# A GAT layer's softmax weights go through a PSUM bank, and two of its small PSUM regions become one

## The chip, the cores and the metric

The kernel runs on one core of a Trainium2 chip. The metric is device time in microseconds (us) from one launch to its end. The engines are TensorE (PE, with its weight loads as PEld), VectorE (DVE), ScalarE (ACT), GpSimd (POOL) and SyncE (SP). Each runs its own instructions in order, and they meet in semaphores.

## The reference

Four graph layers run one after the other over 6,250 nodes of 256 features and 100,000 edges sorted by destination. The change is in layer 0, a GAT layer of 8 heads:

```
h = einsum('nf,fhd->nhd', x, W);  a_src = sum(h*att_src, -1);  a_dst = sum(h*att_dst, -1)
e = leaky_relu(a_src[src] + a_dst[dst], 0.2)
e_exp = exp(e - segment_max(e, dst)[dst]);  denom = segment_sum(e_exp, dst)
alpha = e_exp / (denom[dst] + 1e-16)
out = segment_sum(h[src] * alpha[:, :, None], dst);  x = layernorm(x + relu(out + bias))
```

Layers 1 to 3 (two GCN convolutions, a weighted sum, a four-head attention) follow and are not touched.

## The kernel before, in words

**Steps and groups.** The edges are cut into 832 steps of 128 edges (one per partition), and 16 steps make a group; there are 52 groups. In layer 0 GpSimd gathers a step's 128 rows of 264 numbers from the table `tab_h0` with one indirect DMA (L1031) into a ring of 48 rows, `rows0` in `reg_x`. A row is 256 features, 8 source scores (columns `FEAT:ROW0`) and a one. The DMA of step t waits for the product of step t - 48.

**A step.** VectorE multiplies the 256 features by the 8 weights, each over 32 features (L1354). TensorE multiplies a one-hot 128x128 matrix by the row (L1312, two passes in fp32, written `bank<-reg_x,scratch`) into one of four product banks. VectorE adds that bank to the sums of the node tile (L1337), three steps behind. TensorE may so be up to three steps behind VectorE, and needs the add of step i - 4 before product i.

**The chain.** While a group's 16 steps go on, the weights of the next group are made in small pieces written out by hand, at step k = 0 to 15 of the running group (`chain_scalar`, `chain_tensor`, `chain_vector`):

- k = 0: VectorE caps the source scores (L1210). ScalarE makes the masks (L1091) and the first four one-hots (L1073, L1076; again at k = 2, 4, 5).
- k = 1 to 4: TensorE turns the scores (`turned3`, L1170), ScalarE copies them (L1121), VectorE makes the first running maxima (L1214), TensorE turns their ends (`tails`, L1174, L1175), ScalarE copies those (L1126). Between them TensorE turns the one-hots, four at a time (L1149), ScalarE copies them (L1085), and TensorE multiplies them with the destination scores (`dst0` to `dst3`, L1161).
- k = 6: VectorE carries the maxima from step to step (L1225 to L1238), ScalarE arranges them (L1134 to L1136).
- k = 7: TensorE turns those starting values and spreads the level (`begins`, L1194 and L1196), then does `dst2`; at k = 8 `dst3`. At k = 8 ScalarE copies two columns of it (`begin_col`, L1102), at k = 10 the destination scores (`part`, L1107).
- k = 11: VectorE's second scans (L1241, L1243) start from `begin_col`; then the node's value (L1248), a maximum (L1255) and L1258. At k = 12 TensorE turns that maximum (`larger`, L1178).
- k = 13, 14: VectorE adds `part` (L1262, L1265) and subtracts (L1276, `below`). At k = 14 ScalarE's Exp writes the 128x128 weights into the rows' columns `FEAT:ROW0` (L1114, `weights`). VectorE's multiplies of the next group wait for that.

**PSUM.** There are eight banks: four for products, two for turned one-hots (`bank_t`), one shared by the turned scores (`bank_3`) and the destination scores (`bank_d`), and `psum[7]` for the small transposes and the level (`bank_c`). Finished node tiles are divided, normalised and stored among the steps (`close_vector`, `close_scalar`).

Of the kernel before, what the change touches and what calls it, by code (L numbers as in the profile page):

```python
# [13 lines left out]
P = 128  # L14
NODES = 6250
EDGES = 100000
FEAT = 256
# [242 lines left out]
def build(nc, io):  # L260
    ctx = ExitStack()
    with ctx:
# [82 lines left out]
        s_weighted, s_scaled = signal("rows_weighted"), signal("sums_scaled")  # L345
        s_denscaled = signal("denominators_scaled")
        s_chain = {n: signal(f"{n}_chain") for n in ("vector", "tensor", "scalar")}
        s_far, s_hot4 = signal("distance_made"), signal("four_hots_made")
        s_mixed, s_reverse = signal("message_mixed"), signal("reverse_scaled")
        s_mean, s_bias, s_residual = signal("mean_made"), signal("bias_added"), signal("residual_added")  # L350
# [533 lines left out]
        S, H, D = GROUP, HEADS0, HEAD0_DIM  # L884
        W0_ROW = FEAT + H + 1
        BANKS0, LAG0 = 4, 3
        rows0 = reg_x[:, 0:3 * S * W0_ROW].rearrange("p (s f) -> p s f", f=W0_ROW)
        hots0 = reg_a[:, 0:2 * S * P].rearrange("p (s f) -> p s f", f=P)
        hots_t = reg_a[:, 2 * S * P:2 * S * P + 1024].rearrange("p (s f) -> p s f", s=2)
# [13 lines left out]
        step_masks, tails, states, begins = (cut(2 * P, rows=1) for _ in range(4))  # L903
        assert at_b[0] <= 7488
        level = small[0:1, 400:400 + 4 * H].rearrange("p (k f) -> p k f", k=2)
        bank_t, bank_3, bank_d, bank_c = (psum[4], psum[5]), psum[6][:, 0:3 * P], psum[6][:, 3 * P:4 * P], psum[7]

        h0_a = a_order.named("middle_clear start_clear end_clear")
        h0_v = v_order.named("level begins ones src_less src_below src_at")
        h0_p = p_order.named("src_idx")  # L910
        src_below = reg_w[:, 1280:1280 + POSITIONS]
# [76 lines left out]
        def close_scalar(e, i):  # L988
# [15 lines left out]
            "capped first over_in back_states states level_in level_out second_up second node bent_node larger below_node "  # L1004
            "part_added larger_added shrink_less bent shrink below", GROUPS)
        ch_t = s_chain["tensor"].named(
            "turned3 hots0 hots1 dst0 tails hots2 dst1 hots3 begins dst2 dst3 larger", GROUPS)
        ch_a = s_chain["scalar"].named(
            "upright hot0 kept3 hot1 kept_hot0 step_masks hot2 kept_tails kept_hot1 hot3 begins kept_hot2 kept_hot3 "
            "begin_col part shrink weights", GROUPS)  # L1010
# [54 lines left out]
        def chain_scalar(e, g, k, ahead):  # L1065
# [21 lines left out]
            if ahead:  # L1087
                if k == 0:
                    if g:
                        e.wait_ge(*ch_t.at("turned3", g - 1))  # L1090
                    e.copy(upright[:, 0:2 * P].rearrange("p (k s h) -> p k s h", k=2, h=H),  # L1091
                           bcast(masks[:, :, cols], 3, [P, 2, S, H])).then_inc(*ch_a.done("upright"))
                if k in (0, 2, 4, 5):
                    hot((0, 2, 4, 5).index(k))
                if k == 3:
                    if g:
                        e.wait_ge(*ch_v.at("level_out", g - 1))
                    e.copy(step_masks.rearrange("p (k h s) -> p k h s", k=2, h=H),
                           bcast(run_masks[:, :, cols], 2, [1, 2, H, S])).then_inc(*ch_a.done("step_masks"))
                if k == 8:  # L1100
                    e.wait_ge(*ch_t.at("begins", g))
                    e.copy(begin_col, bank_c[:, 256:258]).then_inc(*ch_a.done("begin_col"))  # L1102
                if k == 10:
                    e.wait_ge(*ch_t.at("dst3", g))
                    if g:
                        e.wait_ge(*ch_v.at("larger_added", g - 1))
                    e.copy(dst_part, bank_d[:, 0:S * H]).then_inc(*ch_a.done("part"))  # L1107
                if k == 11:
                    e.wait_ge(*ch_v.at("below_node", g))
                    e.activation(shrink0, shrink0, ACT.Exp).then_inc(*ch_a.done("shrink"))  # L1110
                if k == 14:
                    e.wait_ge(*ch_v.at("below", g))
                    e.wait_ge(*h0_v.at("ones"))
                    e.activation(group0(g)[0][:, :, FEAT:ROW0], both[:, 0:P].rearrange("p (s h) -> p s h", h=H),  # L1114
                                 ACT.Exp).then_inc(*ch_a.done("weights"))
                return
# [24 lines left out]
        def chain_tensor(e, g, k, ahead):  # L1141
# [23 lines left out]
            if ahead:  # L1165
                if k == 1:
                    e.wait_ge(*ch_a.at("upright", g))
                    e.wait_ge(*ch_v.at("capped", g))
                    for n in range(3):
                        t = e.transpose(bank_3[:, n * P:(n + 1) * P], upright[:, n * P:(n + 1) * P], ident[:, :])  # L1170
                    t.then_inc(*ch_t.done("turned3"))
                if k == 4:
                    e.wait_ge(*ch_v.at("first", g))
                    e.transpose(bank_c[0:1, 0:P], first[:, P - 1:P], ident[:, :])  # L1174
                    e.transpose(bank_c[0:1, P:2 * P], first[:, P:P + 1], ident[:, :]).then_inc(*ch_t.done("tails"))  # L1175
                if k == 12:
                    e.wait_ge(*ch_v.at("larger", g))
                    e.transpose(bank_c[:, 3 * P:4 * P], second[:, 0:P], ident[:, :]).then_inc(*ch_t.done("larger"))  # L1178
                return
            if k == 1:  # L1180
                turn_hots(0)
# [6 lines left out]
            if k == 6:  # L1188
                turn_hots(3)
            if k == 7:  # L1190
                e.wait_ge(*ch_a.at("begins", g))
                e.wait_ge(*h0_v.at("begins"))
                for n in range(2):
                    e.transpose(bank_c[:, 256 + n:257 + n], begins[:, n * P:(n + 1) * P], ident[0:1, 0:1])  # L1194
                e.wait_ge(*ch_v.at("level_in", g))
                e.matmul(bank_c[:, 264:264 + 2 * H], ones_row, level[:, g % 2, :], start=True,  # L1196
                         stop=True).then_inc(*ch_t.done("begins"))
                dst_scores(2)
            if k == 8:
                dst_scores(3)  # L1200

        def leaky(e, v):
            return e.scalar_tensor_tensor(out=v, in0=v, scalar=0.2, in1=v, op0=ALU.mult, op1=ALU.max)
# [1 line left out]
        def chain_vector(e, g, k):  # L1205
# [33 lines left out]
            if k == 11:  # L1239
# [5 lines left out]
                                     ALU.max).then_inc(*ch_v.done("second"))  # L1245
                load_ranks(e, "vector", g * S)
                v = rank_value(e, "vector", g * S)
                e.tensor_tensor(node_both.rearrange("p (k h) -> p k h", k=2),  # L1248
                                bank_c[:, 264:264 + 2 * H].rearrange("p (k h) -> p k h", k=2),
                                bcast(adst[:, bass.DynSlice(v * H, H)], 1, [P, 2, H]),  # L1250
# [9 lines left out]
            if k == 13:  # L1260
# [1 line left out]
                e.tensor_tensor(both[:, 0:P], upright[:, 2 * P:3 * P], dst_part,  # L1262
                                ALU.add).then_inc(*ch_v.done("part_added"))
                e.wait_ge(*ch_t.at("larger", g))
                e.tensor_tensor(both[:, P:2 * P], bank_c[:, 3 * P:4 * P], dst_part,  # L1265
                                ALU.add).then_inc(*ch_v.done("larger_added"))
                e.wait_ge(*ch_a.at("shrink", g))
                e.tensor_scalar(shrink0, shrink0, -1.0, carried[:, g:g + 1], ALU.add,
# [48 lines left out]
        def heads_vector(e):  # L1317
# [24 lines left out]
                            ALU.mult).then_inc(*h0_v.done("src_below"))  # L1342
            e.wait_ge(*h0_v.at("src_below"))
            e.tensor_tensor(src_at_i, src_at, src_below, ALU.add).then_inc(*h0_v.done("src_at"))
            for k in range(S):
                chain_vector(e, 0, k)
            e.wait_ge(*pre_p.at("rest_clear"))
            e.wait_ge(*h0_a.at("end_clear"))
            for i in range(STEPS_PAD):
                g, k = i // S, i % S  # L1350
                row = rows0[:, i % (3 * S), :]
                v = row[:, 0:FEAT].rearrange("p (h d) -> p h d", h=H)
                e.wait_ge(*ch_a.at("weights", g))
                e.tensor_tensor(v, v, bcast(row[:, FEAT:ROW0], 2, [P, H, D]), ALU.mult).then_inc(*weighted0.up)  # L1354
                if g + 1 < GROUPS:
                    chain_vector(e, g + 1, k)
                if i >= LAG0:
                    add(i - LAG0)
                close_vector(e, i)
            for i in range(STEPS_PAD, STEPS_PAD + LAG0 + 16):  # L1360
                if i < STEPS_PAD + LAG0:
                    add(i - LAG0)
# [903 lines left out]
```

## Time and profile before

| | us |
|---|---|
| median of 3 runs | 5281.45 (5277.9 to 5286.8) |
| the profiled execution's own time | 5284.91 |
| its span in the profile | 5283.1 |
| PE busy | 3888.6 (74%) |
| DVE busy | 3504.2 (66%) |
| ACT busy | 2567.7 (49%) |
| POOL busy | 3861.1 (73%) |

The span runs from the first to the last instruction. In the profile "busy" leaves out register and semaphore work, "idle before" is an engine's idle time just ahead of an instruction with what ended it, and L1354 is line 1354 of the kernel. Layer 0's steps lie between about 138 and 1207 us.

### The profile page before, as it was taken

Reading aid. Unit: us, or ns where it says so; the run is one execution under the profiler, and the core shown is the slowest. Engines: PE = TensorE matmul, PEld = TensorE weight load, DVE = VectorE, ACT = ScalarE, POOL = GpSimd, SP = SyncE. Lnnn points to the kernel's source line nnn. Section 1 sums busy time; section 2 is a strip of 40 time slices with the busy share of each in tenths; the row PEclk is TensorE's granted clock in tenths of the full one; section 3 lists DMA queues with packets and bytes.
Section 4 is the critical chain, followed back from the end, with each engine's and each line's share of the span. In section 5 each row is a group of like instructions: output and inputs, shape, how many; then the busy total and the mean of one; then the engine's idle time right before and its main releaser. Section 6 shows DMA issues by size and latency. Waiting matters only on the chain.

```text
span 5283.1 us, 86663 instructions
## 1 busy us (share of the span) xinstructions
PE 3888.6 (74%) x13357; PEld 2393.2 (45%) x13357; DVE 3504.2 (66%) x10780; ACT 2567.7 (49%) x6941; POOL 3861.1 (73%) x3995
## 2 busy tenths in 40 slices
PE   7888888886777777677777777676777657666663
PEld 5666666663444444344434434343334334444442
DVE  5889888885555455354444445666666578888887
ACT  3667666674555555355555551000000166666665
POOL 3777777766777777677777776777777777777775
PEclk8889889898998999777787787878887777777776
DMA  6444444433333333443333333333333322222222
GB/s 171 117 123 123 123 122 122 124 108 106 110 112 111 112 111 112 127 133 112 113 112 111 112 112 100 109 109 109 109 110 109 97 57 57 57 57 57 57 57 67
DMA packets 252627, 549.14 MB, mean 104 GB/s; under 512 B 71467, under 2 KB 136235, under 8 KB 252108
## 3 DMA queue, kind: packets, MB, share of 16 engines
q0 software_dynamic: 178752, 478.34, 33.3%
q1 hardware_dynamic: 45804, 42.37, 2.6%
q10 hardware_dynamic: 27552, 22.89, 1.5%
q8 instruction: 157, 2.57, 0.2%
q14 instruction: 362, 2.97, 0.2%
HBM read 501.16 MB, written 42.15 MB: 103 GB/s over the span
## 4 chain that ended last, share of the span: by engine, by line
POOL 55%; issue 20%; PE 10%; ACT 6%; DVE 4%; DMA 2%; SPq 1%; DVEq 0%; ACTq 0%; POOLq 0%
POOL scratch L1416 41%; POOL scratch L1886 14%; PE bank L1312 5%; PE bank L1161 3%; ACT scratch L1073 2%; DMA scratch<-tab_x,src_idx 1%; DVE reg_acc L1337 1%; PE bank L1149 1%; ACT scratch L1085 1%; DVE reg_x L1354 1%; SPq L872 1%; ACT scratch L1076 1%; DMA scratch<-tab_h,src_idx 1%; POOL reg_x L1031 0%; ACT scratch L1121 0%
## 5 line engine op out<-in xcount | busy, mean ns | idle before, releaser
L1468 PE MATMUL bank<-scratch 128*128 x4986 | 1904.2, 495 | 761.6 <-SPq L1428 407.3
L1478 DVE TENSOR_TENSOR reg_acc<-reg_acc,bank 128x256 f32 x2493 | 1048.1, 420 | 1361.7 <-PE bank L1468 1298.4
L1416 POOL DMA_INDIRECT scratch<-tab_x,src_idx x1566 | 1491.5, 952 | 533.3 <-issue 469.4
L1468 PEld LDWEIGHTS bank<-scratch 128*128 128x128 f32 x4986 | 964.3, 228 | 1602.9 <-issue 1549.0
L1031 POOL DMA_INDIRECT reg_x<-tab_h,src_idx x832 | 831.6, 1000 | 291.0 <-issue 176.7
L1416 POOL DMA_INDIRECT scratch<-tab_h,src_idx x783 | 744.4, 951 | 260.7 <-issue 234.3
L1886 POOL DMA_INDIRECT scratch<-tab_h,src_idx x783 | 741.2, 947 | 248.6 <-issue 237.7
L1937 PE MATMUL bank<-reg_w,scratch 128*128 128x260 f32 x1664 | 637.5, 527 | 286.6 <-issue 185.2
L1437 ACT ACTIVATE scratch<-iota_row,dst_loc 128x128 f32<-128x128 f32 x1662 | 572.1, 392 | 348.2 <-PE bank L1468 333.9
L1312 PE MATMUL bank<-reg_x,scratch 128*128 128x265 f32 x1664 | 577.8, 458 | 73.3 <-DVE reg_x L1354 71.1
L1937 PEld LDWEIGHTS bank<-reg_w,scratch 128*128 128x128 f32 x1664 | 377.3, 253 | 509.7 <-issue 312.1
L1968 ACT ACTIVATE edge_w<-scratch,attr 128x68 f32 x832 | 288.5, 347 | 311.1 <-SPq L1898 281.9
L1312 PEld LDWEIGHTS bank<-reg_x,scratch 128*128 128x128 f32 x1664 | 302.9, 215 | 203.6 <-DVE reg_x L1354 172.1
L1337 DVE TENSOR_TENSOR reg_acc<-reg_acc,bank 128x265 f32 x832 | 355.3, 427 | 45.8 <-PE bank L1312 35.3
L2054 DVE TENSOR_TENSOR reg_acc<-reg_acc,bank 128x260 f32 x832 | 350.3, 421 | 16.1 <-PE bank L1937 3.6
L1354 DVE TENSOR_TENSOR reg_x<-reg_x 128x256 f32<-128x256 f32 x832 | 344.6, 414 | 0.5 <-ACT reg_x L1114 0.5
L1453 DVE TENSOR_SCALAR scratch<-iota_row,dst_loc,edge_w 128x128 f32<-128x128 f32 x831 | 322.3, 389 | 6.1 <-issue 6.1
L1952 ACT ACTIVATE scratch<-iota_row,dst_loc 128x128 f32<-128x128 f32 x832 | 319.8, 386 | 3.4 <-DMA tab_h<-reg_w 1.6
L1787 ACT ACTIVATE adst<-adst,small 128x1 f32<-128x1 f32 x49 | 14.4, 294 | 611.2 <-DVE adst L1830 611.2
L2037 DVE SCALAR_TENSOR_TENSOR reg_w<-scratch,attr,edge_w 128x68 f32<-128x68 f32 x832 | 237.8, 286 | 95.0 <-ACT edge_w L1968 83.4
L2085 DVE TENSOR_TENSOR reg_w<-reg_w,bank 128x520 f32<-128x520 f32 x416 | 286.2, 688 | 0.5
L1442 ACT ACTIVATE scratch<-scratch 128x512 f32<-128x512 f32 x416 | 261.7, 629 | 13.1
(314 smaller groups left out, 4374.9 us busy)
## 6 DMA issues: line engine op xcount, KB each, us to landing
scratch<-tab_x,src_idx POOLq DMA_INDIRECT x1566, 2.8
scratch<-tab_h,src_idx POOLq DMA_INDIRECT x1566, 2.7
reg_x<-tab_h,src_idx POOLq DMA_INDIRECT x832
tab_h<-scratch ACTq DMA_DIRECT2D x7, 924.0 KB, 6.4
reg_x<-in_x SPq DMA_DIRECT2D x7, 896.0 KB, 11.3
reg_w<-in_x SPq DMA_DIRECT2D x49, 128.0 KB, 2.5
tab_x<-reg_acc SPq DMA_DIRECT2D x49, 128.0 KB
tab_xs<-reg_w SPq DMA_DIRECT2D x49, 128.0 KB, 2.7
```

What stands on the lines that cost most here:

```text
L1031: e.indirect_dma_start(rows0[:, t % (3 * S), 0:ROW0], None, tab_h0, bass.IndirectOffsetOnAxis(ap=src_idx[:, t:t + 1], axis=0)).then_inc(*g ...
L1312: e.matmul(psum[i % BANKS0][:, 0:W0_ROW], hots0[:, i % (2 * S), :], rows0[:, i % (3 * S), :], start=True, stop=True).then_inc(*product0.up)
L1337: e.tensor_tensor(v, v, psum[i % BANKS0][:, 0:W0_ROW], ALU.add).then_inc(*added0.up)
L1354: e.tensor_tensor(v, v, bcast(row[:, FEAT:ROW0], 2, [P, H, D]), ALU.mult).then_inc(*weighted0.up)
L1416: e.indirect_dma_start(ring_rows[:, j % SLOTS, :], None, self.table, bass.IndirectOffsetOnAxis(ap=src_idx[:, j:j + 1], axis=0)).then_inc(* ...
L1437: e.activation(ring_hots[:, i % HOTS, :], iota_row[:, :], ACT.Abs, scale=-1.0, bias=dst_loc[:, i:i + 1]).then_inc(*self.far.up)
L1453: e.tensor_scalar(ring_hots[:, i % HOTS, :], iota_row[:, :], dst_loc[:, i:i + 1], edge_w[:, i:i + 1], ALU.is_equal, ALU.mult).then_inc(*se ...
L1468: e.matmul(self.bank(i), ring_hots[:, i % HOTS, :], rows, start=True, stop=True).then_inc(*self.product.up)
L1478: e.tensor_tensor(v, v, self.bank(i), ALU.add).then_inc(*self.added.up)
L1886: e.indirect_dma_start(ring_rows[:, j % SLOTS, 0:ROW3], None, tab_h3, bass.IndirectOffsetOnAxis(ap=src_idx[:, j:j + 1], axis=0)).then_inc( ...
L1937: e.matmul(psum[i % BANKS][:, 0:WIDE3], hots3[:, i % HOTS, :], scaled3[:, i % 4, :], start=True, stop=True).then_inc(*product3.up)
L2054: e.tensor_tensor(v, v, psum[i % BANKS][:, 0:WIDE3], ALU.add).then_inc(*added3.up)
```

## The change

The weights of a group are copied by VectorE (`move_weights`) into `psum[7]`, in one of two halves, at the end of the group before, and the 16 multiplies read them there. The copy that Exp left in the rows stays, for the product's weight columns. The chain's small results move from `psum[7]` to `psum[6]`, the bank that already holds `bank_3` and `bank_d`. With that TensorE does `begins` after `dst3` at k = 8 and no longer before `dst2` at k = 7, ScalarE takes `begin_col` at k = 9, and VectorE waits for ScalarE's `part` ahead of L1248.

```diff
+        weights0 = psum[7][:, 0:2 * S * H].rearrange("p (g s h) -> p g s h", g=2, h=H)
-        bank_t, bank_3, bank_d, bank_c = (psum[4], psum[5]), psum[6][:, 0:3 * P], psum[6][:, 3 * P:4 * P], psum[7]
+        bank_t, bank_3, bank_d, bank_c = (psum[4], psum[5]), psum[6][:, 0:3 * P], psum[6][:, 3 * P:4 * P], psum[6]
...
-                if k == 8:
+                if k == 9:
                     e.wait_ge(*ch_t.at("begins", g))
                     e.copy(begin_col, bank_c[:, 256:258]).then_inc(*ch_a.done("begin_col"))
...
-                    e.transpose(bank_c[:, 3 * P:4 * P], second[:, 0:P], ident[:, :]).then_inc(*ch_t.done("larger"))
+                    e.transpose(bank_c[:, 0:P], second[:, 0:P], ident[:, :]).then_inc(*ch_t.done("larger"))
...
             if k == 7:
+                dst_scores(2)
+            if k == 8:
+                dst_scores(3)
                 e.wait_ge(*ch_a.at("begins", g))
...
-                dst_scores(2)
-            if k == 8:
-                dst_scores(3)
...
                 v = rank_value(e, "vector", g * S)
+                e.wait_ge(*ch_a.at("part", g))
                 e.tensor_tensor(node_both.rearrange("p (k h) -> p k h", k=2),
...
+            def move_weights(g):
+                e.wait_ge(*ch_a.at("weights", g))
+                if g >= 2:
+                    e.wait_ge(*weighted0((g - 1) * S - 1))
+                e.tensor_copy(weights0[:, g % 2], group0(g)[0][:, :, FEAT:ROW0]).then_inc(*moved0.up)
+
             for k in range(S):
                 chain_vector(e, 0, k)
+            move_weights(0)
...
-                e.wait_ge(*ch_a.at("weights", g))
-                e.tensor_tensor(v, v, bcast(row[:, FEAT:ROW0], 2, [P, H, D]), ALU.mult).then_inc(*weighted0.up)
+                e.wait_ge(*moved0(g))
+                e.tensor_tensor(v, v, bcast(weights0[:, g % 2, k, :], 2, [P, H, D]), ALU.mult).then_inc(*weighted0.up)
...
                 close_vector(e, i)
+                if k == S - 1 and g + 1 < GROUPS:
+                    move_weights(g + 1)
```

## Rows read from the trace of the kernel before

**Rows 1.** Page, costliest groups: busy us, mean ns of one, idle before it:

```profile
span 5283.1 us, 86663 instructions
...
L1478 DVE TENSOR_TENSOR reg_acc<-reg_acc,bank 128x256 f32 x2493 | 1048.1, 420 | 1361.7 <-PE bank L1468 1298.4
...
L1031 POOL DMA_INDIRECT reg_x<-tab_h,src_idx x832 | 831.6, 1000 | 291.0 <-issue 176.7
...
L1886 POOL DMA_INDIRECT scratch<-tab_h,src_idx x783 | 741.2, 947 | 248.6 <-issue 237.7
...
L1354 DVE TENSOR_TENSOR reg_x<-reg_x 128x256 f32<-128x256 f32 x832 | 344.6, 414 | 0.5 <-ACT reg_x L1114 0.5
```

**Rows 2.** Who waited, 140 to 1160 us: us in total, times, longest:

```profile
POOL reg_x L1031 <- issue: 163.0, 535, 0.3
...
DVE scratch L1225 <- ACT scratch L1126: 54.0, 37, 3.4
DVE reg_acc L1337 <- PE bank L1312: 35.1, 44, 1.8
DVE scratch L1210 <- DMA reg_x<-tab_h,src_idx: 13.0, 7, 3.2
DVE scratch L1265 <- PE bank L1178: 11.8, 17, 0.9
DVE reg_acc L1337 <- DVE reg_acc L1331: 7.3, 48, 0.2
...
ACT reg_x L1114 <- DVE scratch L1276: 136.8, 48, 4.6
ACT scratch L1107 <- PE bank L1161: 96.6, 43, 4.2
...
PE bank L1312 <- DVE reg_x L1354: 64.0, 127, 2.0
```

**Rows 3.** Windows: busy us (instructions) of PE, PEld, DVE, ACT, POOL, then granted clock:

```profile
140.00:1160.00 1020.00, 870.81 (x4427) 644.10 (x4425) 871.74 (x3125) 703.09 (x1879) 781.56 (x783) 0.89 0.45 122
505.50:525.50 20.00, 15.71 (x91) 11.38 (x90) 17.64 (x64) 14.06 (x42) 15.43 (x16) 1.00 0.54 145
239.20:263.20 24.00, 20.67 (x91) 15.23 (x90) 17.97 (x67) 14.07 (x40) 18.52 (x19) 0.79 0.51 140
```

**Rows 4.** Timeline, 517.7 to 525.3 us, a group at full clock, engine by engine:

```profile
517.76 0.28 PE L1194 MATMUL bank<-ident,scratch 1*128 1x1 f32 x2
...
518.20 1.06 PE L1161 MATMUL bank<-adst,scratch 128*128 x8
...
524.13 0.71 PE L1312 MATMUL bank<-reg_x,scratch 128*128 128x265 f32 x2 [0.90 <-DVE reg_x L1354]
...
518.31 0.16 ACT L1102 COPY scratch<-bank 128x2 f32<-128x2 f32 x1
520.64 0.27 ACT L1107 COPY scratch<-bank 128x128 f32<-128x128 f32 x1 [2.17 <-PE bank L1161]
...
519.65 0.48 DVE L1241 TENSOR_TENSOR_SCAN scratch<-scratch 128x128 f32<-128x128 f32 x1
```

**Rows 5.** Timeline, 253 to 263.5 us, a group at mostly half clock:

```profile
253.51 0.47 DVE L1241 TENSOR_TENSOR_SCAN scratch<-scratch 128x128 f32<-128x128 f32 x1
...
255.81 0.43 DVE L1337 TENSOR_TENSOR reg_acc<-reg_acc,bank 128x265 f32 x1 [0.88 <-PE bank L1312]
...
258.41 0.43 DVE L1337 TENSOR_TENSOR reg_acc<-reg_acc,bank 128x265 f32 x1 [1.50 <-PE bank L1312]
...
260.19 0.29 DVE L1265 TENSOR_TENSOR scratch<-bank,scratch 128x128 f32<-128x128 f32 x1 [0.75 <-PE bank L1178]
...
257.20 0.27 ACT L1107 COPY scratch<-bank 128x128 f32<-128x128 f32 x1 [4.24 <-PE bank L1161]
```

**Rows 6.** Timeline, 519.9 to 541 us: two gathers, and the VectorE instruction beside each:

```profile
524.83 0.95 POOL L1031 DMA_INDIRECT reg_x<-tab_h,src_idx  x1 [0.30 <-issue]
524.86 0.43 DVE L1337 TENSOR_TENSOR reg_acc<-reg_acc,bank 128x265 f32 x1
...
540.26 0.42 DVE L1354 TENSOR_TENSOR reg_x<-reg_x 128x256 f32<-128x256 f32 x1
540.35 1.15 POOL L1031 DMA_INDIRECT reg_x<-tab_h,src_idx  x1 [0.30 <-issue]
```

More of the change, by code:

```diff
@@ L347, in build @@
         s_chain = {n: signal(f"{n}_chain") for n in ("vector", "tensor", "scalar")}
+        s_moved = signal("weights_moved")
         s_far, s_hot4 = signal("distance_made"), signal("four_hots_made")
@@ L905, in build @@
         level = small[0:1, 400:400 + 4 * H].rearrange("p (k f) -> p k f", k=2)
-        bank_t, bank_3, bank_d, bank_c = (psum[4], psum[5]), psum[6][:, 0:3 * P], psum[6][:, 3 * P:4 * P], psum[7]
+        bank_t, bank_3, bank_d, bank_c = (psum[4], psum[5]), psum[6][:, 0:3 * P], psum[6][:, 3 * P:4 * P], psum[6]
         h0_a = a_order.named("middle_clear start_clear end_clear")
+        moved0 = s_moved.take(GROUPS)
         h0_v = v_order.named("level begins ones src_less src_below src_at")
@@ L1006, in build @@
         ch_t = s_chain["tensor"].named(
-            "turned3 hots0 hots1 dst0 tails hots2 dst1 hots3 begins dst2 dst3 larger", GROUPS)
+            "turned3 hots0 hots1 dst0 tails hots2 dst1 hots3 dst2 dst3 begins larger", GROUPS)
         ch_a = s_chain["scalar"].named(
@@ L1264, in chain_vector @@
                 e.wait_ge(*ch_t.at("larger", g))
-                e.tensor_tensor(both[:, P:2 * P], bank_c[:, 3 * P:4 * P], dst_part,
+                e.tensor_tensor(both[:, P:2 * P], bank_c[:, 0:P], dst_part,
                                 ALU.add).then_inc(*ch_v.done("larger_added"))
@@ L1350, in heads_vector @@
                 g, k = i // S, i % S
-                row = rows0[:, i % (3 * S), :]
-                v = row[:, 0:FEAT].rearrange("p (h d) -> p h d", h=H)
-                e.wait_ge(*ch_a.at("weights", g))
-                e.tensor_tensor(v, v, bcast(row[:, FEAT:ROW0], 2, [P, H, D]), ALU.mult).then_inc(*weighted0.up)
+                v = rows0[:, i % (3 * S), 0:FEAT].rearrange("p (h d) -> p h d", h=H)
+                e.wait_ge(*moved0(g))
+                e.tensor_tensor(v, v, bcast(weights0[:, g % 2, k, :], 2, [P, H, D]), ALU.mult).then_inc(*weighted0.up)
                 if g + 1 < GROUPS:
```

## The prediction, made before the changed kernel was run

> **What bounds the kernel now.** I read the page first, for what layer 0 is made of, then the waits, the windows and two timelines. The reader is to see which engine is late where, since the change touches layer 0 alone and the other 4,000 us stay.
>
> GpSimd looks like the bound of layer 0. Its 832 gathers take 1000 ns each [rows 1], and it never sits idle for more than 0.3 us between two [rows 2]: about 1.3 us a step, 16 x 1.3 = 20.8 us a group. But VectorE waits for gathered rows only 7 times, 13.0 us in all [rows 2]. So rows mostly lie ready when they are asked for, and the ring is not full either. The steps themselves go at nearly the same pace: one group took 20.0 us at full clock, one 24.0 us at a granted clock of 0.79 [rows 3]. Two paces are level, so GpSimd alone can give back little, and whatever slows the steps shows at once.
>
> What sets the pace of the steps is a loop over three engines. VectorE is busy 871.7 of 1020 us, TensorE 870.8, ScalarE 703.1 [rows 3]; none is full. ScalarE waits 136.8 us for VectorE's last chain piece L1276 and 96.6 us for TensorE's dst3 [rows 2]. VectorE waits 54.0 us for ScalarE at k = 6 and 35.1 us for products; TensorE waits 64.0 us for VectorE's multiplies [rows 2]. In words: L1276 at k = 14 lets ScalarE go, whose one-hots and copies run until k = 7, which lets TensorE do dst2 and dst3 at k = 7 and 8; VectorE does its second scans at k = 11, and from them comes L1276 again. A delay in this loop is paid in every group.
>
> **The change part by part.**
>
> *The begins behind dst3.* This is the edit that I weigh most. Before, begin_col was copied at 518.31, and VectorE's scan started at 519.65, while TensorE was still on dst3: ScalarE could take part only at 520.64, after 2.17 us of waiting [rows 4]. VectorE so ran its scans over TensorE's backlog. After, the scan needs dst3, then begins, then the copy. TensorE's own work is the same: begins took 518.20 - 517.76 = 0.44 us, which dst2 and dst3 gain and begins then takes again [rows 4]; of it some 0.1 us isn't gained, because the turned one-hots for dst2 come late. So the copy starts near 520.64 + 0.1, takes 0.16 with a handover of 0.05, and the scan starts at 520.95 and not at 519.65: 1.3 us late. From there to the next group VectorE hardly waits, TensorE already waits 0.90 us for VectorE at 524.13, and ScalarE stands waiting for L1276 [rows 2, 4]; so all three move, by 1.3 us.
>
> At half clock the lateness is larger and better covered. Dst3 is done at 257.20, the scan was at 253.51 [rows 5]: 257.20 + 0.2 - 253.51 = 3.9 us. But VectorE then waited 0.88 + 1.50 + 0.75 = 3.13 us for TensorE in the same stretch [rows 5], which a later VectorE no longer does. Net 0.8 us. If all of it is hidden the cost is 0; at most it is the 1.3 us.
>
> Over the stage the granted clock is 0.89 [rows 3], so some four fifths at full clock: 0.8 x 1.3 + 0.2 x 0.8 = 1.2 us a group. Group 0 runs ahead of the steps, 51 remain: 51 x 1.2 = **+61 us**, between 51 x 0.8 = 41 and 51 x 1.3 = 66. As a check, ScalarE's wait for dst3 is 96.6 us over 43 groups, 2.2 each, just that of the group taken as the example.
>
> *The wait for part ahead of L1248.* ScalarE takes part right behind begin_col, 0.27 us [rows 4], while the two scans run 0.48 us and longer: nothing. If closing work of a finished tile falls between them it shows, some tenths in a few groups; that stays inside the bounds.
>
> *The copy of the weights.* 52 copies of 128x128. The nearest row is L1265 of the same size with a bank, 0.29 us [rows 5]. The next multiply has to wait for it, as L1337 waits for L1331, 7.3 us in 48 times, 0.15 us each [rows 2]. 0.44 us x 51 = 22 us of VectorE. It lies behind L1276, so ScalarE's side of the loop doesn't see it; TensorE's side does, through the products ahead of turned3. It waits for Exp no longer than the multiply did (0.5 us in all [rows 1]). Between 0 and 22 I take a third, **+8 us**, as the larger share of TensorE's progress hangs on ScalarE's one-hots.
>
> *The multiply from PSUM.* It was 414 ns with both inputs in SBUF; 128x256 with one input from a bank is 420 ns (L1478), both [rows 1]. 832 x 6 ns = 5 us at most; I take 0. The Trainium skill ("VectorE: DVE Perf Modes", on the TRN2 errata) gives 58 fixed cycles for an SBUF source and 120 for a PSUM source at 0.96 GHz; by it each multiply would be 65 ns dearer, 54 us in all as an estimate. The rows don't bear it out.
>
> *What GpSimd gets.* A gather took 0.95 us beside an add from a bank that starts with it, and 1.15 us where a multiply with two SBUF inputs runs over its start [rows 6]. In layer 3, where the multiplies do read a bank, it is 947 ns in the mean against 1000 here [rows 1]. So the change can take off up to 832 x 53 ns = 44 us of GpSimd, less what other VectorE instructions with two SBUF inputs still hold up. But GpSimd is only waited for 13.0 us [rows 2], and with slower steps not at all: **-13 us**. The Trainium skill ("SBUF — State Buffer", Who interferes with whom) says that a DVE instruction with two SBUF inputs contends with a GpSimd instruction that reads SBUF, and one with a single SBUF input does not; the rows agree. By it alone the stage would be a GpSimd stage and win; the sum doesn't use it.
>
> *The shared bank and the buffers.* The other moved regions add no instruction. Both halves of the weights' bank were last read a group ago: nothing.
>
> Sum: +61 + 8 - 13 = +56 us. The profiled execution took 5284.9, so 5341; it was 3.5 above the median of the runs, so **5337 us** against 5281.5, 1.1% slower.
>
> **The rivals.**
>
> *GpSimd decides, and the stage gets faster.* If the late scans are hidden in all groups, because VectorE's other waits (54.0 + 35.1 + 11.8 us [rows 2]) take up 1.2 us a group (61 us), the pace is GpSimd's, and that rises. Then -13 us, and up to -29 if two thirds of the 44 us reach the end: 5252 to 5268. For it: never a longer idle than 0.3 us on GpSimd. Against it: the largest of these waits is at k = 6, for ScalarE, which itself waited for L1276; it moves along. It decides from the point at which a group's lateness is under some 0.3 us.
>
> *A partial cover.* Half the waits at k = 6 do take it up: 61 - 27 = 34, with the -13 and no price for the copy +21: 5302.
>
> *No change.* -13 against a small loss of the copy and the scans: 5271 to 5292.
>
> *The clock.* TensorE stands idle more, in the middle of a group. The group at a granted clock of 0.79, between the levels of 1.2 and 2.4 GHz, took 24.0 us against 20.0 at full clock [rows 3]. If ten more groups go the same way, +40 on top: 5377. The Trainium skill ("TensorE: Matmul & The Clock Gate", Part 1) says that idle windows put the clock to its lower level; that would turn my forecast into this one. Before, TensorE is at 85% busy and the clock at 0.89 [rows 3], so the effect is there, its size open.
>
> **How the numbers follow.** The forecast has 0.57 and 5337, its own range being 28 us (41 - 13, copy hidden) to 88 (66 + 22, no rows waited for before): 5309 to 5370. The partial cover has 0.10, the clock 0.08, no change 0.10, faster 0.15. To leave out no more than 2 in 10, the range goes down through no change to 5270 and up to 5380; outside lie most of the faster case and the end of the clock's. A measurement of this kernel tells 0.2%, 11 us, from nothing. Slower by more: 0.57 + 0.10 + 0.08 = 0.75; the same 0.10; faster 0.15.
>
> **What the profile of the changed kernel would show.** Right: L1241's counterpart waits for ScalarE's begin_col in nearly every group, 1 to 4 us, where before it did so hardly at all; the wait for products and for the turned maximum shrinks; gathers of layer 0 fall from 1000 ns towards 965 while GpSimd's idle grows, because the ring is full; VectorE no longer waits for gathered rows; the stage ends 50 to 60 us later, and all behind it takes as long as before. Wrong: GpSimd still never idles and the stage is shorter, or the wait at k = 6 has vanished in exchange for the one at k = 11. Wrong in a term: the copy over 0.4 us, the multiply well over 420 ns, or a granted clock of the stage below 0.87.

## The result, and the profile after

The changed kernel takes 5397.78 us in the median of 5 runs (5390.65 to 5398.73), against 5281.45 before (five runs too): 1.0213 times as long, with a 95% interval of 1.0202 to 1.0225, some 112 us. The forecast was 5337, its range ended at 5380. The sign was right, and so was the place: the last add of layer 0 starts at 1319.7 us of the span and not at 1208.5, which is 111 of the 113 us that the span gained. The loss is twice the forecast, and outside its range.

The changed kernel has other line numbers. L1034 is the gather, L1364 the multiply, L1316 the product and L1341 the add. Of the chain, L1200 and L1202 are `begins`, L1105 the copy of `begin_col`, L1110 that of `part`, L1244 and L1246 the second scans, L1252 the node's value, L1259 the maximum, L1181 its turning, L1228 the piece at k = 6 that was L1225, and L1353 the new copy of the weights.

The page of the changed kernel (busy us, mean ns, idle before):

```profile
span 5396.0 us, 86817 instructions
...
L1490 DVE TENSOR_TENSOR reg_acc<-reg_acc,bank 128x256 f32 x2493 | 1048.7, 421 | 1370.5 <-PE bank L1480 1302.6
...
L1034 POOL DMA_INDIRECT reg_x<-tab_h,src_idx x832 | 797.8, 959 | 420.1 <-PE bank L1316 220.9
L1898 POOL DMA_INDIRECT scratch<-tab_h,src_idx x783 | 741.2, 947 | 249.3 <-issue 237.7
...
L1364 DVE TENSOR_TENSOR reg_x<-reg_x,bank 128x256 f32<-128x256 f32 x832 | 340.9, 410 | 2.1 <-issue 0.2
```

The gathers of layer 0 fell from 1000 to 959 ns, and the multiply out of the bank is no dearer than it was [rows 1]: 410 ns. The faster gathers that the change aimed at are there. They aren't used: GpSimd idles 420.1 us ahead of its gathers and not 291.0, and over half of that is waiting for products.

Who waited in the changed kernel, 140 to 1260 us (us in total, times, longest):

```profile
POOL reg_x L1034 <- PE bank L1316: 220.3, 302, 3.3
...
ACT scratch L1105 <- PE bank L1202: 134.7, 49, 5.2
DVE scratch L1244 <- ACT scratch L1105: 105.3, 49, 4.5
PE bank L1316 <- DVE reg_x L1364: 91.5, 154, 2.4
ACT scratch L1113 <- DVE scratch L1262: 71.0, 44, 2.3
...
DVE scratch L1228 <- ACT scratch L1129: 65.4, 41, 3.4
...
DVE scratch L1252 <- issue: 23.2, 45, 0.9
DVE reg_acc L1341 <- PE bank L1316: 10.4, 16, 1.9
...
DVE scratch L1269 <- PE bank L1181: 0.3, 1, 0.3
```

Two rows of the kernel before, 140 to 1160 us, that belong beside them (L1241 is the first of the second scans, L1248 the node's value):

```profile
DVE scratch L1248 <- issue: 6.8, 14, 1.0
...
DVE scratch L1241 <- ACT scratch L1102: 1.8, 3, 1.1
```

Both stretches hold 49 of these scans. Compare [rows 2]. VectorE's second scans now wait for begin_col in all 49, 105.3 us, 2.1 us each, where they waited 1.8 us in three. What it saves is smaller: products 35.1 to 10.4 us, turned maximum 11.8 to 0.3, gathered rows 13.0 to none. The wait at k = 6 didn't shrink, 54.0 to 65.4 us, as the prediction had argued. The wait at the node's value that is put down to no engine ("issue") grew from 6.8 us in 14 groups to 23.2 us in 45.

Windows of the changed kernel, to be read against [rows 3]:

```profile
140.00:1160.00 1020.00, 848.08 (x4036) 617.53 (x4036) 807.62 (x2887) 640.36 (x1713) 688.10 (x719) 0.84 0.41 112
```

In the same 1020 us TensorE made 4036 matmuls and not 4427, all engines are less busy, and the granted clock, a mean over its two levels of 1.2 and 2.4 GHz, is 0.84 and not 0.89.

The timeline of one group of the changed kernel, 510.5 to 525 us, engine by engine, beside [rows 4]:

```profile
515.00 0.95 PE L1164 MATMUL bank<-adst,scratch 128*128 x8
515.88 0.28 PE L1200 MATMUL bank<-ident,scratch 1*128 1x1 f32 x2
516.03 0.37 PE L1202 MATMUL bank<-small 1*128 1x16 f32 x2
...
518.62 0.33 PE L1181 MATMUL bank<-ident,scratch 128*128 128x128 f32 x1 [0.67 <-DVE scratch L1259]
...
516.44 0.16 ACT L1105 COPY scratch<-bank 128x2 f32<-128x2 f32 x1 [2.54 <-PE bank L1202]
...
514.22 0.42 DVE L1364 TENSOR_TENSOR reg_x<-reg_x,bank 128x256 f32<-128x256 f32 x1
516.63 0.48 DVE L1244 TENSOR_TENSOR_SCAN scratch<-scratch 128x128 f32<-128x128 f32 x1 [2.00 <-ACT scratch L1105]
517.03 0.46 DVE L1246 TENSOR_TENSOR_SCAN scratch<-scratch 128x128 f32<-128x128 f32 x1
517.97 0.18 DVE L1252 TENSOR_TENSOR scratch<-bank,adst 128x16 f32<-128x16 f32 x1 [0.48 <-issue]
...
522.88 0.29 DVE L1353 COPY bank<-reg_x 128x128 f32<-128x128 f32 x1
523.20 0.42 DVE L1364 TENSOR_TENSOR reg_x<-reg_x,bank 128x256 f32<-128x256 f32 x1
```

In order of time, one handover is dst3 (515.00), begins (515.88), ScalarE's copy (516.44), the scan (516.63). VectorE had finished its multiply at 514.6 and stood 2.00 us, then 0.48 us more ahead of the node's value, though nothing it waits for by name was open: part was copied at 516.50 to 516.77. TensorE in turn waits for the maximum (L1181).

What was open is a register load. The code has one between the scans and the node's value, and the trace has it on VectorE's sequencer (DVEq), the part that issues its instructions. The first row is the group above in the changed kernel, the second the group of [rows 4] in the kernel before (duration in ns three times, then the start in us twice):

```profile
L841 DVEq TENSOR_LOAD <-step_rows x1: 1096/1096/1096, 516.6 to 516.6; - x1
```

```profile
L840 DVEq TENSOR_LOAD <-step_rows x1: 1097/1097/1097, 519.0 to 519.0; - x1
```

It takes 1.10 us in both. Before, it began at 519.0, with a multiply and both scans still to be done, and was over at 520.1, ahead of the node's value at 520.42. Now it begins at 516.6 with the scan, and the node's value starts only at 517.97.

### The profile page after: what moved, and what is told of

Same layout as the page of the kernel before. It is cut to its first block, busy times and chain, and to the rows that moved or that the text cites. A ratio compares the mean times of both kernels' runs of the same rounds, so it can differ in the third digit from the quotient of the medians.

```text
span 5396.0 us, 86817 instructions
## 1 busy us (share of the span) xinstructions
PE 3953.7 (73%) x13357; PEld 2424.0 (45%) x13357; DVE 3515.8 (65%) x10832; ACT 2567.4 (48%) x6941; POOL 3830.5 (71%) x3995
## 4 chain that ended last, share of the span: by engine, by line
POOL 53%; issue 20%; PE 11%; ACT 5%; DVE 5%; DMA 2%; SPq 1%; DVEq 1%; ACTq 0%; POOLq 0%
POOL scratch L1428 40%; POOL scratch L1898 14%; PE bank L1316 5%; PE bank L1164 4%; ACT scratch L1076 2%; DVE reg_acc L1341 1%; DMA scratch<-tab_x,src_idx 1%; ACT scratch L1088 1%; DVE reg_x L1364 1%; PE bank L1152 1%; SPq L873 1%; DMA scratch<-tab_h,src_idx 0%; PE bank L1173 0%; ACT scratch L1124 0%; ACT L995 0%
## 5 line engine op out<-in xcount | busy, mean ns | idle before, releaser
L1034 POOL DMA_INDIRECT reg_x<-tab_h,src_idx x832 | 797.8, 959 | 420.1 <-PE bank L1316 220.9
L1316 PE MATMUL bank<-reg_x,scratch 128*128 128x265 f32 x1664 | 626.8, 492 | 98.5 <-DVE reg_x L1364 96.8
L1316 PEld LDWEIGHTS bank<-reg_x,scratch 128*128 128x128 f32 x1664 | 322.6, 229 | 246.9 <-DVE reg_x L1364 221.2
L1341 DVE TENSOR_TENSOR reg_acc<-reg_acc,bank 128x265 f32 x832 | 355.3, 427 | 21.4 <-PE bank L1316 10.4
L1364 DVE TENSOR_TENSOR reg_x<-reg_x,bank 128x256 f32<-128x256 f32 x832 | 340.9, 410 | 2.1 <-issue 0.2
L1164 PEld LDWEIGHTS bank<-adst,scratch 128*128 128x128 f32 x1664 | 232.0, 211 | 81.1 <-issue 74.4
```

The source lines that it names most:

```text
L1034: e.indirect_dma_start(rows0[:, t % (3 * S), 0:ROW0], None, tab_h0, bass.IndirectOffsetOnAxis(ap=src_idx[:, t:t + 1], axis=0)).then_inc(*g ...
L1164: m = e.matmul(bank_d[:, t % S * H:(t % S + 1) * H], hots_t[:, c % 2, n * P:(n + 1) * P], adst[:, bass.DynSlice(rank_value(e, "tensor", t) ...
L1316: e.matmul(psum[i % BANKS0][:, 0:W0_ROW], hots0[:, i % (2 * S), :], rows0[:, i % (3 * S), :], start=True, stop=True).then_inc(*product0.up)
L1341: e.tensor_tensor(v, v, psum[i % BANKS0][:, 0:W0_ROW], ALU.add).then_inc(*added0.up)
L1364: e.tensor_tensor(v, v, bcast(weights0[:, g % 2, k, :], 2, [P, H, D]), ALU.mult).then_inc(*weighted0.up)
```

## The experiments

All ratios are to the kernel before, with 95% intervals; us are worked out from them (0.01 is 53 us). A difference of two such ratios is uncertain by 11 to 13 us to either side. The code cuts are short: each names the kernel it starts from.

**e1_order: the order alone.**

```diff
# kernel before: begins behind dst3 (k = 8), banks as they were
-                if k == 8:
+                if k == 9:
                     e.wait_ge(*ch_t.at("begins", g))
# and TensorE's begins moves from ahead of dst_scores(2) to behind dst_scores(3)
```

> The kernel before with the order alone changed: begins behind dst3, begin_col at k = 9; the banks, the multiply from SBUF and L1248 without a wait stay. Theory A (the scans at k = 11 wait for begin_col, and that alone makes the loss): 90 to 120 us slower than before, with the wait of L1241's counterpart for begin_col near the 105 us of the changed kernel. Theory B (the loss is a sum of terms: the order some 60 us, the rest from the copy, from the wait for part and from where TensorE then stands): 50 to 80 us slower.

1.0155 (1.0138 to 1.0172), 82 us. Its waits, 140 to 1240 us:

```profile
DVE scratch L1241 <- ACT scratch L1102: 100.9, 49, 5.4
...
DVE scratch L1248 <- issue: 20.8, 49, 0.9
```

The order makes nearly three quarters of the loss, with no weights' bank and no shared bank. The size is at the edge between the two theories; the wait is theory A's. The wait put down to issue is there too, in 49 groups and not 14. VectorE's wait for gathered rows, 13.0 us before, is gone here as well, though the gathers still take 992 ns: the slower steps took it away, not faster gathers.

**e2_bank: order, shared bank and the wait for part; no weights' bank.**

```diff
# changed kernel, move_weights left out
-                e.wait_ge(*moved0(g))
-                e.tensor_tensor(v, v, bcast(weights0[:, g % 2, k, :], 2, [P, H, D]), ALU.mult).then_inc(*weighted0.up)
+                e.wait_ge(*ch_a.at("weights", g))
+                e.tensor_tensor(v, v, bcast(rows0[:, i % (3 * S), FEAT:ROW0], 2, [P, H, D]), ALU.mult).then_inc(*weighted0.up)
```

> The changed kernel with the weights read from the rows in SBUF again, without the copy: order, shared bank and the wait for part ahead of L1248 stay. Against e1_order it adds the wait for part and the shared bank. Theory A: within 10 us of e1_order, so 90 to 120 us slower than before, and level with the changed kernel. Theory B: some 20 to 30 us slower than e1_order, because part is taken by ScalarE only behind begin_col, and less than the changed kernel by the copy's 10 to 22 us. Gathers of GpSimd are back near 1000 ns in both, but cost nothing since the ring is full.

1.0175 (1.0158 to 1.0192): some 11 us over e1_order, with overlapping intervals, and 20 us under the changed kernel. Theory A's level with the changed kernel is out.

**e3_copy: the copy alone, into SBUF.**

```diff
# kernel before
+        weights0 = cut(2 * S * H).rearrange("p (g s h) -> p g s h", g=2, h=H)   # SBUF
+                if k == S - 1 and g + 1 < GROUPS:
+                    move_weights(g + 1)
# and the multiplies read weights0
```

> The kernel before with the copy of the weights alone, into a spare 128x256 piece of SBUF, from which the multiplies read; order and banks stay. The forecast's term for the copy was 0 to 22 us, 8 taken. Theory A: 0 to 15 us. Theory B: 15 to 30 us, as VectorE has 0.44 us more in each of 51 groups in the stretch that TensorE waits for. GpSimd's gathers stay near 1000 ns, since the multiply has two inputs in SBUF as before.

1.0012 (0.9999 to 1.0025): 6 us, at the edge of what can be told from nothing, and 13 us at the interval's upper end. It is theory A's size. Of the 22 us at which the copy was bounded it costs about a third here. The gathers stay at 990 ns, so it is the bank, and not the copy, that speeds them. One thing differs from the change: this copy into SBUF takes 217 ns in the median, the one into the bank 286.

**e4_first: begins ahead of dst2 again, in the shared bank.**

```diff
# changed kernel, k = 7: begins, then
+                e.wait_ge(*ch_a.at("begin_col", g))
                 dst_scores(2)
# ScalarE at k = 7: begin_col, then kept_hot3
```

> The changed kernel with begins ahead of dst2 again, in the shared bank: dst2 now waits until ScalarE has copied begin_col, which it does ahead of kept_hot3. The scans don't wait for dst3 any more; L1248 still waits for part. Theory A: the loss goes nearly all, 0 to 30 us slower than before. Theory B: half of it stays, 40 to 70 us slower, because VectorE now stops at L1248 for part, some 1.5 us later in the same step, and because dst2 waits for begin_col.

1.0129 (1.0112 to 1.0146), 68 us: theory B, and 44 us less than the changed kernel. VectorE no longer waits at the scans; it waits some 0.9 us of work further on, at the node's value, for part. Dst2 now also waits for the copy of begin_col, 21.1 us in all:

```profile
DVE scratch L1252 <- ACT scratch L1107: 80.0, 50, 4.2
...
PE bank L1163 <- ACT scratch L1140: 21.1, 51, 1.3
```

**e6_part: the wait for part alone.**

```diff
# kernel before, ahead of L1248
+                e.wait_ge(*ch_a.at("part", g))
```

> The kernel before with one wait more: VectorE waits for ScalarE's part ahead of L1248; nothing else. Theory of a loop paid wherever VectorE stands behind dst3 in step 11: the node comes 1 us later than it did (part was done about 1.1 us after it in most groups), so 25 to 60 us slower, a part of the order's 86 us. Rival, that only the scans' wait counts as it holds 1.4 us of VectorE's work: 0 to 15 us.

1.0069 (1.0045 to 1.0093), 36 us (24 to 49), from one wait in one instruction of 0.15 us that reads 16 columns:

```profile
DVE scratch L1249 <- ACT scratch L1107: 76.8, 47, 3.8
```

So two different waits cost, each of which makes VectorE stand behind dst3 in step 11. Behind the order the same wait, with the shared bank, adds some 11 us (e2_bank less e1_order), which can't be told from nothing: VectorE already stands there.

**e5_node: neither scans nor node behind dst3.**

```diff
# e4_first, and:
+            if k == 12:        # VectorE: the node's value moves here
# TensorE: the turned maximum behind the product of step 12, waiting for node
+                e.wait_ge(*ch_v.at("node", g))
```

> As e4_first (begins ahead of dst2, which waits for the copied begin_col), and the node's value, which has to wait for part, is read one step later, at k = 12, with the turned maximum behind it and behind TensorE's product. So neither scans nor node stand behind dst3, while weights in their bank, copy and shared bank stay. If the loss is all of VectorE standing behind dst3: -15 to +15 us against before. If a term from the copy, the bank and the handovers stays: +20 to +45 us.

1.0201 (1.0187 to 1.0215), 106 us: a miss. Part of the wait moved once more, to L1270, VectorE's add of the turned maximum; VectorE waits more for products too; and the node's value (L1256) still waits 25.1 us for part:

```profile
DVE reg_acc L1342 <- PE bank L1317: 38.3, 63, 2.0
DVE scratch L1270 <- PE bank L1203: 36.5, 30, 1.8
...
DVE scratch L1256 <- ACT scratch L1107: 25.1, 32, 1.0
```

It joins two edits, the later node and the later turning, and doesn't tell which costs.

**e7_load: the register load early.** `load_ranks` loads 16 registers of a group's tile ranks, out of which L1248 takes an address.

```diff
# changed kernel
+            if k == 9:
+                load_ranks(e, "vector", g * S)
             if k == 11:
...
-                load_ranks(e, "vector", g * S)
                 v = rank_value(e, "vector", g * S)
```

> The changed kernel with VectorE's load of the group's 16 rank registers moved from between the scans and L1248 to step 9. In the changed kernel VectorE waits 23.2 us at its L1252 in 45 times put down to issue, against 6.8 us in 14 times before. If that is the register load, which shows once VectorE has run dry at the scans: the 23 us go and the kernel gets 12 to 22 us faster than the changed one (some +95 to +105 us against before). If it is hidden or moves elsewhere: within 5 us of the changed kernel.

1.0161 (1.0146 to 1.0177), 0.0052 under the changed kernel: 27 us, by the medians 31, more than the 12 to 22 expected. The wait of 23.2 us put down to issue was the register load: it is gone from there. The load isn't free at its new place either, where 8.6 us in 20 times are put down to issue ahead of the add. The scans' wait fell to 82.1 us as well:

```profile
DVE scratch L1246 <- ACT scratch L1105: 82.1, 49, 4.2
...
DVE reg_acc L1342 <- issue: 8.6, 20, 0.9
```

**e9_order_load and e11_before_load: the same in e1_order and in the kernel before.** The diff is that of e7_load.

> e1_order with the load of VectorE's rank registers at step 9, as in e7_load. If the register load is a term of its own once the scans stand: 20 to 30 us faster than e1_order, so +55 to +65 us against before, which is what the forecast had for the order without it (+61). If its gain in e7_load hung on the bank or on the wait for part: within 8 us of e1_order.

> The kernel before with the load of the rank registers at step 9 alone. VectorE waited 6.8 us in 14 times at L1248, put down to issue. If the load is what it waits for there: 3 to 10 us faster. If it was covered before: within 5 us. Either way far less than the 31 us of e7_load, since VectorE didn't run dry at the scans before.

e9_order_load: 1.0104 (1.0087 to 1.0121), again 27 us under e1_order. e11_before_load: 1.0006 (0.9997 to 1.0015), nothing. Moving the same load is worth 27 us where the scans stand and nothing where they don't. The two loads of 1.10 us above fit this: before, VectorE had work queued while the load went on; right behind a wait it has too little.

**e8_busy: work for TensorE that goes nowhere.** Nothing of the computation is changed; the products are overwritten.

```diff
# changed kernel, ahead of the product of step i
+                if k in (12, 13, 14, 15) and g + 1 < GROUPS:
+                    e.wait_ge(*added0(i - BANKS0))
+                    for n in range(2):
+                        e.matmul(psum[i % BANKS0][:, 0:P], ident[:, :], ident[:, :], start=True, stop=True)
```

> The changed kernel with work for TensorE that goes nowhere: ahead of the product in steps 12 to 15 two 128x128 products of the identity into the bank that the product then overwrites. It fills time in which TensorE waits for VectorE. In the changed kernel the stage's granted clock is 0.84, before it was 0.89. If the lower clock is an effect of the new idle time and costs much: the granted clock rises by 0.03 or more and the time falls by 5 to 25 us against the changed kernel. If the clock isn't what costs: the clock may rise, the time is the same or up to 20 us longer.

1.0189 (1.0173 to 1.0204), 13 us under the changed kernel by the ratios, 19 by the medians; the intervals overlap a little, while each of its runs is faster than each of the changed kernel's. The window of the stage:

```profile
140.00:1160.00 1020.00, 876.40 (x4850) 672.59 (x4851) 824.14 (x2951) 656.41 (x1756) 704.78 (x736) 0.93 0.42 115
```

The granted clock rose from 0.84 to 0.93, and a pass of the product took 435 ns in the mean and not 492. VectorE's wait at the scans fell from 105.3 to 93.5 us, the one at k = 6 from 65.4 to 51.9.

**e12_before_busy: the same products in the kernel before.**

> The kernel before with e8_busy's idle products for TensorE in steps 12 to 15. In e8_busy the stage's granted clock rose from 0.84 to 0.93 and the time fell by some 18 us. If a low clock after idle time cost before too: the clock rises from 0.89 to 0.94 and the time falls by 5 to 15 us. If TensorE's order is tighter before, and the idle products stand in its way: 0 to 20 us slower.

1.0005 (0.9995 to 1.0016), no change, although the clock rose from 0.89 to 0.92 and a pass of the product fell from 459 to 435 ns:

```profile
140.00:1160.00 1020.00, 917.58 (x5268) 729.43 (x5267) 880.59 (x3157) 711.43 (x1899) 779.93 (x789) 0.92 0.44 123
```

**e15_load_busy: early load and idle products in the changed kernel.** The diff is that of e7_load and of e8_busy.

> The changed kernel with both the early register load of e7_load and the idle products of e8_busy. If the two are separate terms they add: 31 + 18 = 49 us faster than the changed kernel, +65 to +75 us against before. If the clock's gain came from time that the register load left idle: within 8 us of e7_load, +77 to +93 us.

1.0119 (1.0103 to 1.0136): 22 us under e7_load by the ratios, 16 by the medians, and 50 us under the changed kernel. The rival, within 8 us of e7_load, is out by the ratios: load and idle products are separate terms and add. The granted clock is 0.91 against 0.86 in e7_load:

```profile
140.00:1160.00 1020.00, 903.25 (x4962) 701.80 (x4963) 840.13 (x3018) 669.21 (x1792) 725.10 (x754) 0.91 0.43 117
```

**e10_level: the whole change with nothing of VectorE behind dst3.**

```diff
# e4_first, load early, and:
-                e.copy(begin_col, bank_c[:, 256:258])
+                e.copy(begin_col, bank_c[:, 256:280])       # the level too
-                e.wait_ge(*ch_a.at("part", g))
-                                bank_c[:, 264:264 + 2 * H].rearrange("p (k h) -> p k h", k=2),
+                                begin_col[:, 8:8 + 2 * H].rearrange("p (k h) -> p k h", k=2),
# TensorE, ahead of turning the maximum at k = 12
+                    e.wait_ge(*ch_a.at("part", g))
```

> All of the change (weights' bank, copy, shared bank), but nothing of VectorE stands behind dst3: begins goes ahead of dst2, ScalarE copies begin_col and the level in one copy of 24 columns, and the node's value reads that copy, so no wait for part; the rank registers are loaded at step 9. If the waits behind dst3 and the register load are the whole of the loss: -20 to +10 us against before. If weights' bank and copy cost as forecast (8 us) and dst2's wait for the copy costs too: +10 to +35 us.

1.0107 (1.0092 to 1.0123), 56 us: a miss, if half of the changed kernel's loss. Its waits:

```profile
DVE reg_acc L1342 <- PE bank L1317: 79.2, 87, 1.8
...
ACT scratch L1140 <- PE bank L1199: 61.3, 46, 3.9
...
PE bank L1163 <- ACT scratch L1140: 18.3, 48, 1.3
```

VectorE's scans and node no longer stand behind dst3, but now ScalarE stands at begin_col (L1140), for begins, with its last copy of one-hots behind it, and TensorE stands for the copy of begin_col ahead of dst2. I read this as the round trip moved from VectorE to the two others; VectorE waits for products in its place.

**e13_three and e14_three_lag2: the weights' bank with the chain of before.** The bank is taken from the products, which keep three.

```diff
# e3_copy
+        weights0 = psum[3][:, 0:2 * S * H].rearrange("p (g s h) -> p g s h", g=2, h=H)
-        BANKS0, LAG0 = 4, 3
+        BANKS0, LAG0 = 3, 3        # e14_three_lag2: 3, 2
```

> The weights' bank and its copy with the chain of before untouched: the bank is the fourth product bank, so three are left; the add stays three steps behind, the product of step i waits for the add of step i - 3. GpSimd's gathers should fall from 1000 to 960 ns. If the weights' bank gives nothing or little while the steps hold: -10 to +15 us, three banks costing some of it. If the third bank's loss ties TensorE to VectorE: +30 to +80 us, which then says nothing of the weights' bank.

> As e13_three with the adds two steps behind the multiplies, so that the bank of step i is free one step earlier. TensorE has one step less to be late by. If TensorE's backlog at dst3 is what VectorE ran over: 20 to 60 us slower than before, with more waits of VectorE for products. If three banks only hurt through the late release: faster than e13_three.

1.0165 (1.0151 to 1.0178) and 1.0125 (1.0108 to 1.0142): 87 and 66 us, both above the ranges expected (to 80 and 60). Releasing the bank one step earlier gives back some 21 us. The gathers fell here too (e13_three):

```profile
L1034 POOL DMA_INDIRECT reg_x<-tab_h,src_idx x832 | 799.8, 961 | 365.4 <-PE bank L1315 166.3
```

But in e13_three TensorE's products wait for adds, a wait that neither the kernel before nor the changed one has:

```profile
PE bank L1315 <- DVE reg_acc L1340: 147.0, 202, 2.5
```

Weights' bank and missing product bank can't be told apart in them. No version here beats the kernel before.

## Why the prediction was right in sign and wrong in size

By the ratios the loss of 0.0213, 112 us, comes apart along one path of kernels: the order with the register load moved away 0.0104, 55 us (e9_order_load); the load, once VectorE stands, 0.0051, 27 us (e1_order less e9_order_load; the changed kernel less e7_load gives the same); shared bank and wait for part 0.0020, 11 us; weights' bank and copy 0.0038, 20 us. Each of the last three is uncertain by 11 to 13 us. Along another path the terms have another size: alone, the wait for part costs 36 us and a copy into SBUF 6.

- **The step that failed** is "From there to the next group VectorE hardly waits". It left out what stands between the scans and L1248, the register load. The load was in the code and in the trace, as 14 waits put down to issue, and no term of the sum had it. Its cover was the work queued on VectorE, and the edit took that away: 27 us. With it the order, the term of the begins at +61 with -13 for the rows, 48 us net, measures 82 us. With the load moved the order costs 55 us.
- **What the term got right.** In VectorE's own waits, the scans stand 103.5 us more, and the products and the turned maximum take 36.2 us less: 67 us, where the forecast had 61. Gathered rows give the 13 us back, as forecast. What comes on top is 16 us put down to issue, 11 us at k = 6, and some 16 us for 51 copies. That 55 lies so close to 48 is in part luck: the forecast took its group times at a granted clock of 0.89, and e9_order_load ran at 0.86.
- **That VectorE behind dst3 costs: shown,** by e1_order and by e6_part, where one wait without any work costs 36 us. That the stage is a loop over three engines is a reading of who waits for whom, and the runs agree with it.
- **The lateness itself** was 1.3 us in the forecast, 2.0 us of standing in the group shown. From dst3's end (515.95) to the scan (516.63) it is 0.68 us, what the forecast's parts give as well. The rest is VectorE's lead: it began its last multiply 1.73 us before dst3 ended, 1.28 us in [rows 4] (519.32 to 520.60), where the forecast had dst3 end 0.34 us earlier. Why the lead grew isn't shown; the group of [rows 4] had no waits for products that could have gone. The copy of the weights took 0.32 us from its start to the next multiply, less than the 0.44 priced.
- **The wait for part, priced at nothing: open.** The two scans were to cover ScalarE's 0.27 us, and in the group shown they do (part was done at 516.77, L1252 started at 517.97). Over the stage the changed kernel waits there for ScalarE 2.4 us in 4 groups, the "tenths in a few groups" of the prediction. The 11 us that e2_bank has for bank and wait together aren't beyond the intervals.
- **The copy at +8:** 6 us in e3_copy, with a shorter copy. In the changed kernel the weights' bank and copy come to 20 us, near the upper of the bounds of 0 and 22. VectorE's chain is already late there; whether the rest is the copy in a tighter loop, the writing into PSUM or the clock stays open.
- **The multiply from PSUM at 0: right,** 410 ns against 414. The Trainium skill ("VectorE: DVE Perf Modes", The TRN2 errata) has 62 cycles more for a PSUM source; neither row shows them for this form.
- **GpSimd: the gathers came as forecast,** 959 ns, towards 965. No run has them alone, but e2_bank, with gathers of 996 ns, is 20 us faster than the changed kernel, so their gain doesn't even pay for copy and bank. The rule of the Trainium skill on two SBUF inputs ("SBUF — State Buffer", Who interferes with whom) agrees with the gathers of e13_three too, 961 ns, against 1000 before. The pair of [rows 6] alone didn't show it: a multiply with two SBUF inputs ran 0.12 us into the shorter gather as well (524.53 to 524.95). The means do.
- **The rival of the clock came on top of the forecast** and not instead of it. The granted clock of the stage fell to 0.84, below the 0.87 named as the mark. Idle products bring it to 0.93 and give 13 us in the changed kernel and 22 us behind e7_load; in the kernel before they give nothing. That idle time of TensorE goes with a lower clock is shown by e8_busy, where filling it raised the clock. That the gain comes through the clock, and that it shows only where the loop has no slack at TensorE, is how I read it; no run changes the clock alone. How many of the 112 us are clock isn't additive to the terms above, since each of these runs has its own (0.85 in e1_order, 0.86 in e9_order_load).
- **The rest of the kernel stayed:** in the pass that follows, a product pass takes 495 ns in both and an add 421 ns against 420 [rows 1], and the gathers of layer 3 take 947 ns in both.

## What to carry to other kernels

Before a resource is shared to make room, list what each new order lets stand behind what: here the order forced by one shared bank, with the register load behind it, cost 82 of 112 us, and the engine that was relieved, GpSimd, was hardly waited for. Where an edit makes an engine wait, look at what comes right behind the wait on it, register loads included: this one was hidden only while work was queued. Handing the same wait on to another instruction or engine gave back half of the loss at best, as e4_first and e10_level show; ask which round trip is gone altogether.

## What the runs showed of the hardware

- A load of 16 registers takes VectorE's sequencer 1.10 us, in both kernels. With a multiply and two scans queued, the group shown had no idle time from it; right behind a wait it shows as 0.5 us put down to issue (23.2 us in 45 times). Moving it ahead of the wait is worth 27 us of the kernel's time (e7_load, e9_order_load), and nothing where the wait isn't (e11_before_load: 1.0006).
- 128x128 products of the identity, two in each of four steps of sixteen, raised the granted clock from 0.84 to 0.93. The changed kernel was 13 us faster with them, the kernel before no different (0.89 to 0.92).
- The indirect gathers take 959 to 965 ns in the mean in the kernels whose multiplies read one input from PSUM, and 989 to 1000 ns in those whose multiplies read both from SBUF; the adds, which read a bank, were there in either case.
- A VectorE copy of 128x128 takes 286 ns in the median from SBUF into PSUM (the changed kernel) and 217 ns from SBUF into SBUF (e3_copy).
